# A post-norm decoder block on one NeuronCore: another order for the second half's projection tiles, weight requests and FFN products

## The chip, the cores and the metric

The kernel runs on one core of a Trainium2 chip. The metric is the device time of one execution in microseconds; before the change it is 2226.97 us, the median of three runs (2224.86 to 2243.2). Engines are called by their names in the profile: PE is TensorE, PEld its weight loads, DVE is VectorE, ACT is ScalarE, POOL is GpSimd and SP is the queue that issues all DMAs.

## What is computed

x is (4, 1024, 512), the context (4, 2048, 512). Three sublayers, each followed by a layer norm over the 512 features:

```python
x = layernorm(x + attention(x))          # q, k, v each from two linear maps, 32 head slots of 16; then one projection, wo
x = layernorm(x + xattn(x, ctx, fside))  # see below
x = layernorm(x + ffn(x))                # x rounded to 8-bit integers, times a ternary 512 x 512 matrix, + bias

# xattn: of the 1024 rows of x, rows 0..511 are h (z1h) and rows 512..1023 are c (z1c)
xp = concatenate([z0h, z1h], axis=2)                  # h shifted by one column
out = uss + conv(xp, weight, kernel 2) + bias         # (2048, 512) weights for each of two taps, uss is the context
it, ot, gt, ft = sigmoid, sigmoid, tanh, sigmoid of the four quarters of out
ct = ft * z0c + it * gt                               # z0c: c shifted by one column
ht = ot * tanh(ct)
return concatenate([ht, ct], axis=1)
```

So the convolution contracts over the 512 rows of h and needs all of them; c is needed only for the elementwise product with the gate ft.

## The kernel before

All fp32 products are made as three matmuls of high and low parts (`product3`). The program has four stages: `combine` and `project` make q, k and v, `attend` does the attention with TensorE nearly always busy, and `finish` does everything from the output projection on. Only `finish` (from about 1751 us of the span) and two lines of loads for it are touched.

`finish` treats the four batches in two pairs (p = 0, 1; bi = 0, 1 within a pair). A batch has TT = 8 row tiles t of 128 rows; KC = 4, so tiles t 0..3 are h and t 4..7 are c. For each pair it does:

- **Projection** (`wo_stage`): 16 tiles of 12 matmuls, in the order of positions `pos` that `wo_tile` maps to (bi, t). The left operand is in two buffers `o_hi`/`o_lo`, one half of each for bi = 0 and one for bi = 1, each half holding four tiles; `load_o`/`next_o` load a half (1 MB high, 1 MB low). Results go to six PSUM banks (`WO_BANKS`). VectorE adds x (to which GpSimd has added the bias, `add_wob`) and computes the statistics (`start_norm`: three operations), GpSimd the inverse deviation (`inv_std`), ScalarE applies the norm (`apply`). y, the tile between them, has a ring of four.
- **The convolution's rows** (`first_term`, `last_term`, `high_parts`, `low_parts`): from each h tile the minimal-filtering form of a two-tap convolution makes three half-width operands, each in two parts (`x_wino`). `tmp` uses the buffers of gate 0 and 1 in between.
- **Convolution** (`convs`): CONVS = 16 sets s. Set s belongs to m = s // 4 (which 128 rows) and gate g = s % 4; it has 4 channel blocks c of 9 matmuls (`conv_block`), and needs 1.5 MB of weights in one of two buffers (`load_w`). VectorE adds the result to the context in `gates` (two operations of 1024 columns), ScalarE does the sigmoid or tanh. After g = 2 the new c and after g = 3 the new h are made and normalised (keys "c", "h"); then the next context (`load_ctx`) may come in.
- **FFN**: 16 blocks q (`ffn_tile`). VectorE rounds (`rounded`), ScalarE makes integers (`integers`), TensorE transposes (`turn`), ScalarE copies (`copy_turned`), TensorE multiplies (`ffn`, bank 7), VectorE reads it (`out_of_ffn`), ScalarE normalises into the output (`apply_ffn`). In set s VectorE does `out_of_ffn(s-6)` and `rounded(s-4)` before the set's own sums. TensorE does `turn(s-5)` before the last channel block of set s and `ffn(s-5)` after it. x of the second pair is loaded into the place of block q when block q is out (`next_x`).

Six FFN blocks (10 to 15) of the first pair are left when its sets end; they are fitted into the projection of the second pair. The tables at the head of `finish` say where: `ORDER[p]` is the order in which all engines but TensorE take the tiles, `FFN_AT` says before which entry of it an `ffn_part` stands, `FFN_SLOT` the same for TensorE's positions, `X_AT` when GpSimd adds the bias to an x tile. `place` numbers all normalisations in program order, which is how the ring's users agree.

Each engine runs its own instructions in order and waits on semaphores. On SP too each request waits in order, so a request stands behind all waits ahead of it.

## Time and profile before

| | us |
|---|---|
| median of three runs | 2226.97 |
| lowest, highest | 2224.86, 2243.2 |
| the profiled execution | 2238.76 |
| its span, first to last instruction | 2236.8 |
| TensorE, VectorE, ScalarE, GpSimd busy | 2120.3, 1658.8, 1314.4, 487.8 |
| projection and rows, first pair | 1752.6 to 1807.3 |
| sets 0 to 15, first pair | 1807.3 to 1972.4 |
| projection, rows, FFN blocks 10 to 15 | 1974.5 to 2038.8 |
| sets 0 to 15, second pair | 2038.8 to 2200.6 |
| end | 2236.8 |

The profile is of one execution. A row of a timeline gives the start in us from the span's start, the duration, the engine, the line, the operation with output and inputs, and in brackets the engine's idle time before it with what ended it. Matmuls overlap, so a group's duration is a little more than their pace. A landing is counted from the request to the arrival of the last byte.

### The profile page before, as it was taken

To read this page: it belongs to the slowest core of one execution; us is meant where nothing else is said; L and a number is where in the kernel's file an instruction comes from. 1 tells how busy PE (TensorE), PEld (TensorE's weight loads), DVE (VectorE), ACT (ScalarE), POOL (GpSimd) and SP (SyncE) were. 2 spreads that over 40 slices of the span, in tenths; PEclk is the share of its full clock that TensorE was granted. 3 is DMA by queue.
4 is the path that set the end of the run, shared out by engine and by line. 5 is a ranking of instruction groups with operands and counts; after the bars stand their busy time and mean duration, and the time that the engine had idled before them with its cause. 6 is when DMAs were issued, how large, how long until landed. Compare 5 with 4: busy or idle time off the path is not lost. (4 is left out here: it accounts for less than half of the span.)

```text
span 2236.8 us, 40038 instructions
## 1 busy us (share of the span) xinstructions
PE 2120.3 (95%) x11304; PEld 1190.4 (53%) x11304; DVE 1658.8 (74%) x1725; ACT 1314.4 (59%) x2429; POOL 487.8 (22%) x972
## 2 busy tenths in 40 slices
PE   8999996999999999999999999999999979987995
PEld 3788883444444444444444444444443667766773
DVE  3333326888999999999999999999995357785776
ACT  0121120777888888888888888888887233443344
POOL 0000000112121221221221221221221533464234
PEclk9999995999999999999999999999998789999997
DMA  4355547354565664664665664654654646753562
GB/s 155 95 168 150 151 149 97 59 131 105 112 138 100 125 138 101 124 138 100 125 138 101 124 138 101 124 138 101 124 130 158 245 168 264 258 195 140 220 231 76
DMA packets 205963, 315.20 MB, mean 141 GB/s; under 512 B 105169, under 2 KB 105169, under 8 KB 193617
## 3 DMA queue, kind: packets, MB, share of 16 engines
q1 hardware_dynamic: 205904, 314.47, 54.2%
q8 instruction: 31, 0.51, 0.1%
q14 instruction: 28, 0.22, 0.0%
HBM read 211.06 MB, written 101.19 MB: 140 GB/s over the span
## 5 line engine op out<-in xcount | busy, mean ns | idle before, releaser
L517 DVE TENSOR_REDUCE neg_max<-psum 128x1 f32<-128x1024 f32 x1024 | 1205.2, 1220 | 143.9 <-PE psum L405 143.6
L497 ACT ACTIVATE probs<-psum 128x512 f32<-128x512 f32 x2048 | 1066.3, 604 | 326.3 <-PE psum L423 323.8
L423 PE MATMUL psum<-q_op,k_op 50*128 50x512 f32 x2048 | 765.7, 456 | 6.2 <-ACT probs L497 3.9
L423 PEld LDWEIGHTS psum<-q_op,k_op 50*128 50x128 f32 x2048 | 359.1, 194 | 593.5 <-ACT probs L497 569.9
L405 PE MATMUL psum<-k_op,q_op 48*128 48x512 f32 x2048 | 633.2, 489 | 21.6 <-DMA k_op<-qk_parts_dram 14.1
L432 PE MATMUL psum<-probs,v_op 128*32 128x512 f32 x4096 | 557.7, 617 | 1.7
L405 PEld LDWEIGHTS psum<-k_op,q_op 48*128 48x128 f32 x2048 | 390.0, 315 | 51.9 <-DVE neg_max L517 19.3
L149 PE MATMUL psum<-x_wino,conv_w 128*128 128x512 f32 x1152 | 287.5, 407 | 29.5 <-DMA conv_w<-conv_w_parts_dram 14.9
L149 PEld LDWEIGHTS psum<-x_wino,conv_w 128*128 128x128 f32 x1152 | 222.2, 195 | 81.3 <-issue 32.6
L567 POOL CAST neg_max_parts<-neg_max 128x8 fp32r<-128x8 f32 x128 | 24.5, 191 | 809.3 <-DVE neg_max L517 809.3
L432 PEld LDWEIGHTS psum<-probs,v_op 128*32 128x32 f32 x4096 | 83.1, 108 | 132.5 <-issue 74.3
L230 ACT ACTIVATE qk_parts<-psum,qk_bias 128x512 fp32r<-128x512 f32 x64 | 44.1, 689 | 166.0 <-PE psum L149 166.0
L243 DVE SCALAR_TENSOR_TENSOR qk_parts<-psum,qk_bias,qk_parts 128x512 fp32r<-128x512 f32 x64 | 48.0, 750 | 120.1 <-ACT qk_parts L230 120.1
L557 POOL COPY v_op<-values 128x256 f32 (+1 forms) x64 | 25.5, 398 | 455.3 <-issue 344.6
L1049 ACT ACTIVATE x<-y,neg_mean_rstd,rstd 128x512 f32<-128x512 f32 x64 | 52.1, 816 | 103.6 <-POOL neg_mean_rstd L963 103.6
L149 PE MATMUL psum<-x_hi,w_hi 128*128 128x512 f32 x256 | 101.9, 398 | 5.0 <-ACTq L224 5.0
L1323 DVE TENSOR_TENSOR gates<-psum,gates 128x1024 f32<-128x1024 f32 x32 | 38.9, 1216 | 90.3 <-PE psum L149 90.3
L149 PE MATMUL psum<-x_lo,w_hi 128*128 128x512 f32 x256 | 101.7, 397 | 0.0
L149 PE MATMUL psum<-x_hi,w_lo 128*128 128x512 f32 x256 | 101.6, 397 | 0.0
L1105 ACT ACTIVATE gates<-gates,conv_bias 128x1024 f32<-128x1024 f32 x32 | 36.7, 1151 | 93.3 <-DVE gates L1326 93.2
L683 POOL TENSOR_TENSOR o_raw<-o_raw,recips 128x512 f32<-128x512 f32 x32 | 41.0, 1282 | 175.9 <-DMA recips<-recips_dram 175.9
L958 POOL TENSOR_TENSOR var_eps<-mean_var,eps 128x1 f32<-128x1 f32 x96 | 30.8, 321 | 200.9 <-DVE mean_var L1228 200.7
(98 smaller groups left out, 1655.4 us busy)
## 6 DMA issues: line engine op xcount, KB each, us to landing
q_op<-qk_parts_dram SPq DMA_DIRECT2D x384, 128.0 KB, 4.0
conv_w<-conv_w_parts_dram SPq DMA_DIRECT2D x32, 1536.0 KB, 7.9
qk_parts_dram<-qk_parts SPq DMA_DIRECT2D x128, 256.0 KB, 3.1
k_op<-qk_parts_dram SPq DMA_DIRECT2D x384, 64.0 KB, 3.8
conv_w_parts_dram<-conv_w_parts SPq DMA_DIRECT2D x16, 1536.0 KB, 6.1
attended_dram<-out SPq DMA_DIRECT2D x64, 256.0 KB, 2.1
attended_parts_dram<-o_parts SPq DMA_DIRECT2D x128, 128.0 KB, 2.2
gates<-in_ctx_dram SPq DMA_DIRECT2D x32, 512.0 KB, 4.3
```

The lines of the kernel that those rows point to most:

```text
L149: mm = nc.tensor.matmul(out, left, right, start=(first and i == 0), stop=(last and i == n - 1))
L230: nc.scalar.activation(parts[j % 4][:, 0, :], bank[j % 6], ACT.Identity, bias=qk_bias[:, j // KC, j % KC:j % KC + 1]).then_inc(qk_hi, 1)
L243: nc.vector.scalar_tensor_tensor(out=parts[j % 4][:, 1, :], in0=bank[j % 6], scalar=qk_bias[:, j // KC, j % KC:j % KC + 1], in1=parts[j % ...
L405: return nc.tensor.matmul(s1_bank[t % 2][:, lane * HALF:(lane + 1) * HALF], qop[i][r, b, t:S:QT], kop[i][r, b, :], start=True, stop=True)
L423: nc.tensor.matmul(s2_bank[cell % RING], kop[i][r, j // 2, n // 2 * P:(n // 2 + 1) * P], qop[i][r, j // 2, j % 2 * HALF:(j % 2 + 1) * HALF ...
L432: mm = nc.tensor.matmul(pv_bank[32 * j:32 * j + 32, :], vop[k % 2][:, j // 2 * QT + kt, :], probs[n % DEEP][:, j, :], start=(n == 0), stop ...
L497: nc.scalar.activation(probs[n % DEEP][:, j, :], s2_bank[cell % RING], ACT.Exp, scale=SCALE).then_inc(exp_done, 1)
L517: nc.vector.tensor_reduce(mx[b][:, t:t + 1], s1_bank[t % 2][:], AX_X, ALU.max, negate=True).then_inc(maxed, 1)
L683: nc.gpsimd.tensor_tensor(norm["o"][:], norm["o"][:], norm["den"][:], ALU.mult).then_inc(norm["o_made"], 1)
L1049: A.activation(dst, y[r][:], ACT.Identity, bias=nmr[:, r:r + 1], scale=rstd[:, r:r + 1]).then_inc(normed, 1)
L1105: A.activation(gin[:, g, :, :], gin[:, g, :, :], ACT.Tanh if g == 1 else ACT.Sigmoid, bias=cb[:, col:col + 1]).then_inc(gate_out, 1)
L1323: steps.done(V.tensor_tensor(both, bank[4 + s % 2].rearrange("p (b i a) -> p b i a", b=2, a=1).broadcast_to([P, 2, HF, 2]), both, ALU.add))
```

## The change

- `WO_TILES` replaces the arithmetic of `wo_tile`: positions 0 to 7 are now the h tiles, (0,0), (0,1), (1,0), (1,1), (0,2), (1,2), (0,3), (1,3), and 8 to 15 the c tiles. `load_o` loads the h half first, the first x tiles loaded in `attend` are those of the new positions 0 to 3, and `next_o` asks for the halves of the c tiles when seven and eight tiles are multiplied (before: four and eight). Row making moves to the entries behind each h tile. `WO_BANKS` is turned so that the banks of set 0 are free after thirteen tiles; TensorE waits for thirteen tiles before set 0 and sixteen before set 1. A wait is added on VectorE before c is used.
- Sets 0 and 1 run one after the other (before: blocks 0 to 2 of both, then block 3 of both).
- SP asks for the weights of set s + 2 before the contexts that follow set s - 1 (before: before the contexts that follow set s, ahead of the next weights).
- TensorE multiplies FFN block s - 6 behind the first channel block of set s (before: block s - 5 behind set s).
- Between the pairs single tables (`O_AT`, `R_AT`, `TURN_AT`, `FFN_AT`, `COPY_AT`) replace `ffn_part` and `FFN_SLOT`, so that rounding, turning, copying and multiplying a block each have a position of their own. ScalarE copies block 11 within set 15.

```diff
+    WO_BANKS = (4, 2, 3, 5, 0, 1)
+    WO_TILES = ((0, 0), (0, 1), (1, 0), (1, 1), (0, 2), (1, 2), (0, 3), (1, 3)) + \
+        tuple((bi, t) for bi in range(2) for t in range(KC, TT))
+    ORDER = (tuple(range(TILES)), (0, 1, 2, 3, 4, 5, 8, 9, 6, 10, 7, 11, 12, 13, 14, 15))
...
+    FFN_AT = ({}, {1: 10, 2: 11, 5: 12, 6: 13, 7: 14, 8: 15})
...
 def next_o(p, n):
-    sp.wait_ge(wo_full, p * TILES + 4 * n - 4)
+    sp.wait_ge(wo_full, p * TILES + (4 * n - 4 if n < 2 else n + 5))
...
 def convs(p):                                   # SP
     for s in range(CONVS):
-        m, g = s // 4, s % 4
-        if p * CONVS + s + 2 < 2 * CONVS and s + 2 < CONVS:
+        if s + 2 < CONVS:
             sp.wait_ge(conv_full, p * CONVS + s + 1)
             load_w(p * CONVS + s + 2)
+        if s > 0:
+            next_ctx(p, s - 1)
...
-        if m < KC - 1 and g == 2:
-            sp.wait_ge(cell_made, p * KC + m + 1)
-            load_ctx(p, m + 1, 2)
...
                 next_o(0, 2)
-                for pos in range(8, TILES):
-                    load_x(0, *wo_tile(pos))
...
 def convs(p):                                   # TensorE
-    for s in range(2):
-        pe.wait_ge(wo_out, p * TILES + TILES - 1 + s)
-        pe.wait_ge(cw_in[s], (p * CONVS // 2 + 1) * DMA)
-        for c in range(KC - 1):
-            conv_block(p, s, c)
-    for s in range(2):
-        conv_block(p, s, KC - 1)
-    for s in range(2, CONVS):
+    for s in range(CONVS):
         n = p * CONVS + s
-        pe.wait_ge(gate_in, n - 1)
+        if s < 2:
+            pe.wait_ge(wo_out, p * TILES + 13 + 3 * s)
+        else:
+            pe.wait_ge(gate_in, n - 1)
         pe.wait_ge(cw_in[n % 2], (n // 2 + 1) * DMA)
         for c in range(KC):
+            if c == 1 and s >= 6:
+                ffn(p, s - 6)
             if c == KC - 1 and s >= 5:
                 turn(p, s - 5)
             conv_block(p, s, c)
-        if s >= 5:
-            ffn(p, s - 5)
+    turn(p, CONVS - 5)
...
 def wo_stage(p):                                # VectorE
     for i, pos in enumerate(ORDER[p]):
-        if i in FFN_AT[p]:
-            ffn_part(p - 1, FFN_AT[p][i])
+        if i in O_AT[p]:
+            out_of_ffn(p - 1, O_AT[p][i])
+        if i in R_AT[p]:
+            rounded(p - 1, R_AT[p][i])
         out_of_wo(p, pos)
...
+        if wino_of(p, i - 2) is not None:
+            low_parts(p, wino_of(p, i - 2))
+        if wino_of(p, i - 1) is not None:
+            first_term(p, wino_of(p, i - 1))
```

How the order moves, first on SP at the first pair's projection (`o_hi` and `o_lo` are the attention rows, `x` the residual tiles, `o_parts` the last attention results). Before:

```order
L655 DMA recips<-recips_dram 128x1x512 [waits recips_out]
L697 DMA o_hi<-attended_parts_dram 128x4x512 [waits wo_full]
L697 DMA o_lo<-attended_parts_dram 128x4x512
L839 DMA x<-in_x_dram 128x512 x8
L670 DMA attended_parts_dram<-o_parts 32x2x512 [waits o_lo_made]
L670 DMA attended_parts_dram<-o_parts 32x2x512 x3
L697 DMA o_hi<-attended_parts_dram 128x4x512 [waits wo_full]
L697 DMA o_lo<-attended_parts_dram 128x4x512
L852 DMA conv_w<-conv_w_parts_dram 128x3072 [waits conv_w_stored]
L852 DMA conv_w<-conv_w_parts_dram 128x3072
```

After:

```order
L656 DMA recips<-recips_dram 128x1x512 [waits recips_out]
L848 DMA x<-in_x_dram 128x512 x8
L698 DMA o_hi<-attended_parts_dram 128x4x512 [waits wo_full]
L698 DMA o_lo<-attended_parts_dram 128x4x512
L698 DMA o_hi<-attended_parts_dram 128x4x512 [waits wo_full]
L698 DMA o_lo<-attended_parts_dram 128x4x512
L671 DMA attended_parts_dram<-o_parts 32x2x512 [waits o_lo_made]
L671 DMA attended_parts_dram<-o_parts 32x2x512 x3
L861 DMA conv_w<-conv_w_parts_dram 128x3072 [waits conv_w_stored]
L861 DMA conv_w<-conv_w_parts_dram 128x3072
```

The eight x tiles now stand ahead of the first attention rows, and the two pairs of attention rows stand next to each other ahead of the store.

SP again, from the first weights requested within the sets (sets 2 and 3 of the first pair) on; `gates` is the context. Before:

```order
L852 DMA conv_w<-conv_w_parts_dram 128x3072 [waits conv_full] x2
L697 DMA o_hi<-attended_parts_dram 128x4x512 [waits wo_full,o_parts_stored]
L697 DMA o_lo<-attended_parts_dram 128x4x512
L852 DMA conv_w<-conv_w_parts_dram 128x3072 [waits conv_full]
L848 DMA gates<-in_ctx_dram 128x2x512 [waits cell_made]
L848 DMA gates<-in_ctx_dram 128x2x512 [waits var_made,tanh_made]
L852 DMA conv_w<-conv_w_parts_dram 128x3072 [waits conv_full]
L848 DMA gates<-in_ctx_dram 128x2x512 [waits h_made]
L848 DMA gates<-in_ctx_dram 128x2x512 [waits var_made]
L852 DMA conv_w<-conv_w_parts_dram 128x3072 [waits conv_full]
L697 DMA o_hi<-attended_parts_dram 128x4x512 [waits wo_full]
L697 DMA o_lo<-attended_parts_dram 128x4x512
```

After:

```order
L861 DMA conv_w<-conv_w_parts_dram 128x3072 [waits conv_full] x2
L698 DMA o_hi<-attended_parts_dram 128x4x512 [waits wo_full,o_parts_stored]
L698 DMA o_lo<-attended_parts_dram 128x4x512
L861 DMA conv_w<-conv_w_parts_dram 128x3072 [waits conv_full] x2
L857 DMA gates<-in_ctx_dram 128x2x512 [waits cell_made]
L857 DMA gates<-in_ctx_dram 128x2x512 [waits var_made,tanh_made]
L861 DMA conv_w<-conv_w_parts_dram 128x3072 [waits conv_full]
L857 DMA gates<-in_ctx_dram 128x2x512 [waits h_made]
L857 DMA gates<-in_ctx_dram 128x2x512 [waits var_made]
L698 DMA o_hi<-attended_parts_dram 128x4x512 [waits wo_full]
L698 DMA o_lo<-attended_parts_dram 128x4x512
L861 DMA conv_w<-conv_w_parts_dram 128x3072 [waits conv_full] x2
```

The third and fourth weight requests (sets 4 and 5) now follow each other with no context between them, and so on by four.

TensorE in sets 6 and 7 of the first pair (`tern` is the FFN's matrix, `ident` the identity of a turn). Before:

```order
L149 MATMUL psum<-x_wino,conv_w 128x512 [waits conv_w_in0,gate_in]
L149 MATMUL psum<-x_wino,conv_w 128x512 x26
L1136 MATMUL psum<-ident,x_int 128x128 [waits tp_out,xi_made]
L1136 MATMUL psum<-ident,x_int 128x128 x3
L149 MATMUL psum<-x_wino,conv_w 128x512 x9
L1146 MATMUL psum<-tern,x_int_t 128x512 [waits ffn_out,tp_out]
L1146 MATMUL psum<-tern,x_int_t 128x512 x3
L149 MATMUL psum<-x_wino,conv_w 128x512 [waits conv_w_in1,gate_in]
L149 MATMUL psum<-x_wino,conv_w 128x512 x26
L1136 MATMUL psum<-ident,x_int 128x128 [waits tp_out,xi_made]
L1136 MATMUL psum<-ident,x_int 128x128 x3
```

After:

```order
L149 MATMUL psum<-x_wino,conv_w 128x512 [waits conv_w_in0,gate_in]
L149 MATMUL psum<-x_wino,conv_w 128x512 x8
L1168 MATMUL psum<-tern,x_int_t 128x512 [waits tp_out]
L1168 MATMUL psum<-tern,x_int_t 128x512 x3
L149 MATMUL psum<-x_wino,conv_w 128x512 x18
L1158 MATMUL psum<-ident,x_int 128x128 [waits tp_out,xi_made]
L1158 MATMUL psum<-ident,x_int 128x128 x3
L149 MATMUL psum<-x_wino,conv_w 128x512 x9
L149 MATMUL psum<-x_wino,conv_w 128x512 [waits conv_w_in1,gate_in]
L149 MATMUL psum<-x_wino,conv_w 128x512 x8
L1168 MATMUL psum<-tern,x_int_t 128x512 [waits ffn_out,tp_out]
L1168 MATMUL psum<-tern,x_int_t 128x512 x3
```

The FFN product has moved from the end of a set to behind the first nine matmuls of the next.

## Rows read from the trace of the kernel before

**Rows 1.** The view of waits, TensorE, 1750 to 2237 us: in total, times, longest.
```profile
PE psum L149 <- DMA conv_w<-conv_w_parts_dram: 14.9, 5, 4.6
PE psum L1146 <- DVE y L1257: 14.7, 8, 2.0
```

**Rows 2.** Timeline of TensorE, 1800 to 1846 us: start, us, instructions, idle before.
```profile
1807.27 19.44 PE L149 MATMUL psum<-x_wino,conv_w 128*128 128x512 f32 x72 [7.99 <-DVE x_wino L1289]
1831.36 14.83 PE L149 MATMUL psum<-x_wino,conv_w 128*128 128x512 f32 x52 [4.65 <-DMA conv_w<-conv_w_parts_dram]
```

**Rows 3.** Timelines of VectorE: its first read after sets 2, 6, 10, 14.
```profile
1842.60 1.22 DVE L1323 TENSOR_TENSOR gates<-psum,gates 128x1024 f32<-128x1024 f32 x1 [13.02 <-PE psum L149]
...
1880.18 1.23 DVE L1323 TENSOR_TENSOR gates<-psum,gates 128x1024 f32<-128x1024 f32 x1 [5.95 <-PE psum L149]
...
1921.50 1.23 DVE L1323 TENSOR_TENSOR gates<-psum,gates 128x1024 f32<-128x1024 f32 x1 [4.44 <-PE psum L149]
...
1963.16 1.22 DVE L1323 TENSOR_TENSOR gates<-psum,gates 128x1024 f32<-128x1024 f32 x1 [3.89 <-PE psum L149]
...
2072.04 1.22 DVE L1323 TENSOR_TENSOR gates<-psum,gates 128x1024 f32<-128x1024 f32 x1 [11.73 <-PE psum L149]
...
2109.28 1.23 DVE L1323 TENSOR_TENSOR gates<-psum,gates 128x1024 f32<-128x1024 f32 x1 [4.45 <-PE psum L149]
...
2150.09 1.22 DVE L1323 TENSOR_TENSOR gates<-psum,gates 128x1024 f32<-128x1024 f32 x1 [4.44 <-PE psum L149]
...
2191.42 1.23 DVE L1323 TENSOR_TENSOR gates<-psum,gates 128x1024 f32<-128x1024 f32 x1 [4.45 <-PE psum L149]
```

**Rows 4.** Timeline of the DMA queue, 1855 to 1863 us: weights after two contexts.
```profile
1861.57 1.34 SPq L852 DMA_DIRECT2D conv_w<-conv_w_parts_dram  x1
```

**Rows 5.** Timeline of TensorE, 1880 to 1980 us: FFN products between sets.
```profile
1891.52 1.60 PE L1146 MATMUL psum<-tern,x_int_t 128*128 128x512 bf16 x4 [1.99 <-DVE y L1257]
1892.56 7.78 PE L149 MATMUL psum<-x_wino,conv_w 128*128 128x512 f32 x27
...
1902.53 1.04 PE L1146 MATMUL psum<-tern,x_int_t 128*128 128x512 bf16 x4
...
1911.92 1.04 PE L1146 MATMUL psum<-tern,x_int_t 128*128 128x512 bf16 x4
```

**Rows 6.** Timeline of VectorE, 1890 to 1902 us: two readings of FFN products.
```profile
1890.63 0.75 DVE L1257 SCALAR_TENSOR_TENSOR y<-psum,scale,x 128x512 f32<-128x512 f32 x1
...
1901.13 0.75 DVE L1257 SCALAR_TENSOR_TENSOR y<-psum,scale,x 128x512 f32<-128x512 f32 x1
```

**Rows 7.** Tile views, landing: o_lo issued at 1767, at 2008; then all weights.
```profile
DMA to landing us min/median/max: 7.2/7.2/7.2
...
DMA to landing us min/median/max: 13.5/13.5/13.5
...
DMA to landing us min/median/max: 6.2/7.9/16.1
```

**Rows 8.** Timelines between the pairs, TensorE 1977.60 and 2038.82, the others VectorE.
```profile
1977.60 0.60 PE L1136 MATMUL psum<-ident,x_int 128*128 128x128 bf16 x4 [2.08 <-ACT x_int L1056]
...
2024.26 0.74 DVE L1257 SCALAR_TENSOR_TENSOR y<-psum,scale,x 128x512 f32<-128x512 f32 x1
...
2029.49 0.68 DVE L1247 TENSOR_TENSOR y<-psum,x 128x512 f32<-128x512 f32 x1
...
2031.11 0.43 DVE L1284 TENSOR_TENSOR x_wino<-x,x_wino 128x256 fp32r<-128x256 f32 x1
...
2032.50 0.69 DVE L1247 TENSOR_TENSOR y<-psum,x 128x512 f32<-128x512 f32 x1
...
2037.12 0.88 DVE L1284 TENSOR_TENSOR x_wino<-x,x_wino 128x256 fp32r<-128x256 f32 x1
...
2038.82 5.83 PE L149 MATMUL psum<-x_wino,conv_w 128*128 128x512 f32 x18 [6.40 <-DVE x_wino L1289]
```

**Rows 9.** Timeline of TensorE, 2200 to 2237 us: the product of block 11.
```profile
2215.13 1.89 PE L1146 MATMUL psum<-tern,x_int_t 128*128 128x512 bf16 x4 [9.51 <-ACT x_int_t L1062]
```

More of the change, by code:

```diff
@@ L376, in slot @@
                         for t in range(KC):
-                            sp.dma_start(late["x_first"][:, t, :], x_nat[0, (KC + t) * P:(KC + t + 1) * P, :])\
+                            b, row = t // 2, t % 2 * P
+                            sp.dma_start(late["x_first"][:, t, :], x_nat[b, row:row + P, :])\
                                 .then_inc(late["x_in"], DMA)
@@ L721, in finish, with wino_of @@
     RING = 4
-    WO_BANKS = (0, 1, 4, 2, 3, 5)
-    ORDER = (tuple(range(TILES)), (0, 1, 2, 4, 5, 6, 3, 8, 9, 7, 10, 11, 12, 13, 14, 15))
-    FFN_AT = ({}, {0: 16, 3: 17, 4: 18, 6: 19, 8: 20, 11: 21})
-    FFN_SLOT = ({}, {0: 16, 3: 17, 5: 18, 7: 19, 9: 20, 11: 21})
-    X_AT = {2: 9, 6: 12, 7: 10, 9: 13, 10: 11, 11: 14, 14: 15}
+    WO_BANKS = (4, 2, 3, 5, 0, 1)
+    WO_TILES = ((0, 0), (0, 1), (1, 0), (1, 1), (0, 2), (1, 2), (0, 3), (1, 3)) + \
+        tuple((bi, t) for bi in range(2) for t in range(KC, TT))
+    ORDER = (tuple(range(TILES)), (0, 1, 2, 3, 4, 5, 8, 9, 6, 10, 7, 11, 12, 13, 14, 15))
+    O_AT = ({}, {0: 10, 1: 11, 3: 12, 4: 13, 6: 14, 7: 15})
+    R_AT = ({}, {0: 12, 1: 13, 2: 14, 3: 15})
+    TURN_AT = ({}, {4: 12, 5: 13, 6: 14, 7: 15})
+    FFN_AT = ({}, {1: 10, 2: 11, 5: 12, 6: 13, 7: 14, 8: 15})
+    COPY_AT = ({}, {1: 12, 2: 13, 3: 14, 4: 15})
+    X_AT = {2: 10, 3: 11, 4: 9, 6: 12, 7: 14, 8: 13, 9: 15}
     def wo_tile(pos):
-        return pos // 4 % 2, pos % 4 + (KC if pos < 8 else 0)
+        return WO_TILES[pos]
+    def wino_of(p, i):
+        return ORDER[p][i] if 0 <= i < TILES and ORDER[p][i] < 2 * KC else None
     def ffn_tile(q):
@@ L743, in finish @@
         for i, pos in enumerate(ORDER[p]):
-            if i in FFN_AT[p]:
-                takes("ffn", p - 1, FFN_AT[p][i] - 6)
+            if i in O_AT[p]:
+                takes("ffn", p - 1, O_AT[p][i])
             takes("wo", p, pos)
@@ L919, in _ @@
                 convs(0)
+                for n in range(CONVS, CONVS + 2):
+                    sp.wait_ge(conv_full, n - 1)
+                    load_w(n)
                 next_x(10)
@@ L922, in _ @@
                 next_x(11)
-                next_o(1, 2)
-                store(0, 11)
-                next_x(12)
-                for n in range(CONVS, CONVS + 2):
-                    sp.wait_ge(conv_full, n - 1)
-                    load_w(n)
                 sp.wait_ge(var_made, place["h", 0, KC - 1, 1] + 1)
@@ L931, in _ @@
                     load_ctx(1, 0, g)
+                store(0, 11)
+                next_x(12)
+                store(0, 12)
                 next_x(13)
-                store(0, 12)
+                next_o(1, 2)
+                store(0, 13)
+                next_x(14)
+                store(0, 14)
                 next_o(1, 3)
-                next_x(14)
-                store(0, 13)
                 next_x(15)
-                store(0, 14)
                 store(0, 15)
@@ L965, in add_wob @@
                 def add_wob(p, bi, t):
-                    pool.wait_ge(x_in[bi * TT + t], (p if bi == 0 and t >= KC else p + 1) * DMA)
+                    pool.wait_ge(x_in[bi * TT + t], (p if (bi, t) in WO_TILES[:KC] else p + 1) * DMA)
                     G.tensor_tensor(x_at(bi, t), x_at(bi, t), wob[:], ALU.add).then_inc(x_wob, 1)
@@ L1090, in wo_stage @@
                     for i, pos in enumerate(ORDER[p]):
-                        if i in FFN_AT[p]:
-                            ffn_part(p - 1, FFN_AT[p][i])
+                        if i in COPY_AT[p]:
+                            copy_turned(p - 1, COPY_AT[p][i])
+                        if i in R_AT[p]:
+                            integers(p - 1, R_AT[p][i])
+                        if i in O_AT[p]:
+                            apply_ffn(p - 1, O_AT[p][i])
                         apply(x_at(*wo_tile(pos)), "wo", p, pos)
-                        if i >= 9:
-                            high_parts(p, (i - 9) // KC, (i - 9) % KC)
-                    high_parts(p, 1, 3)
+                        if wino_of(p, i - 1) is not None:
+                            high_parts(p, wino_of(p, i - 1))
                 def convs(p):
@@ L1148, in ffn @@
                     mm.then_inc(ffn_full, 1)
-                def ffn_part(p, s):
-                    if s > CONVS:
-                        ffn(p, s - 6)
-                    if s - 5 < TILES:
-                        turn(p, s - 5)
                 def wo_stage(p):
                     for pos in range(TILES):
-                        if pos in FFN_SLOT[p]:
-                            ffn_part(p - 1, FFN_SLOT[p][pos])
-                        n = pos // 4
-                        if pos % 4 == 0:
-                            pe.wait_ge(late["o_in"][n % 2], (2 * p + n // 2 + 1) * (2 * DMA))
+                        if pos in FFN_AT[p]:
+                            ffn(p - 1, FFN_AT[p][pos])
+                        if pos in TURN_AT[p]:
+                            turn(p - 1, TURN_AT[p][pos])
+                        bi, t = wo_tile(pos)
+                        n = bi + (2 if t >= KC else 0)
+                        pe.wait_ge(late["o_in"][bi], (2 * p + n // 2 + 1) * (2 * DMA))
                         if pos >= 6:
@@ L1211, in _ @@
                 convs(1)
-                for s in range(CONVS, CONVS + 6):
-                    ffn_part(1, s)
+                for q in range(CONVS - 6, TILES):
+                    ffn(1, q)
+                    if CONVS - 4 <= q + 1 < TILES:
+                        turn(1, q + 1)
             @block.vector
```

92 lines of the change are left out of this document (49 added, 43 removed).

## The prediction

> **What bounds the kernel now.** I read the view of TensorE's waits over the last 485 us first, then the timelines of TensorE, VectorE and the DMA queue around each wait, because the diff leaves everything before 1751 us alone. In that last part TensorE has the most work, and what can be won is its idle time. Two families of waits stand out [rows 1]: 14.9 us for convolution weights in five waits, and 14.7 us for FFN rows that VectorE had not yet read in eight waits. A third is the wait for the convolution's rows: 7.99 us before the first convolution and 6.40 us before the second pair's [rows 2, 8]. Each long pause also costs clock. The 72 matmuls after the 7.99 us pause took 19.44 us [rows 2], against 16.3 at the undisturbed pace. That pace is 9.39 us for a whole set (36 convolution matmuls, a turn and an FFN product, no wait) [rows 5], of which I give 8.15 to the 36 matmuls and 2.72 to a projection tile of 12. After the 4.65 us pause 52 matmuls took 14.83 us [rows 2], 3.0 more than 52 x 0.227. So a pause of about 5 us costs 5 plus 2 to 3. I call T2, T6, T10 and T14 the end of a pair's sets 2, 6, 10 and 14 (counted from 0), which is where VectorE starts on its sums; [rows 3] hold these for both pairs: 1842.60, 1880.18, 1921.50, 1963.16, and 2072.04, 2109.28, 2150.09, 2191.42.
>
> **Step 1, first pair up to T2 (now 1842.60).** Gone: the 7.99 us wait for rows, because they are made from tiles 0 to 7 while tiles 8 to 15 still multiply; and the 4.65 us weight wait with its slow 3.0 us. Sets 0 and 1 now run one after the other, so the weights of set 2 are asked for 8.15 us before they are needed rather than when both are nearly done. New: both halves of the attention rows are now asked for only when seven and eight tiles are done, so tile 8 waits for them. TensorE starts at 1752.6, loses 3 us to the clock as now, ends tile 6 at about 1774.8 and tile 7 at 1777.5. The second of the two requests leaves at 1775.3. The nearest rows for its landing are 7.2 us (little else in flight) and 13.5 us (amid weights) [rows 7]. At 1775 the eight x tiles, now asked for ahead of it, have mostly landed, so I take 7.2: TensorE goes on at 1782.5, after 5.0 us idle. Eight tiles take 21.8 us and the clock 2.5: 1806.8. VectorE has then emptied thirteen tiles by about 1800 (a tile with its rows takes it 3.0 us, from one reading to the next in [rows 8]), so the convolution follows at once. Three sets at 8.15: 1831.3. **Gain 11.3** (5.0 if landing takes 13.5).
>
> **Step 2, sets 3 to 6 of either pair (T2 to T6).** Now 37.6 and 37.2 us [rows 3]. Two weight waits lie in the first, since the queue stood behind the context's waits (weights issued at 1861.57 [rows 4], where set 4 had ended at 1842.6 + 16.5 = 1859.1). With weights ahead: 8.2 + 8.2 + 8.4 + 9.4 = 34.2. Gains 3.4 and 3.0. In the first pair one request for set 7 comes right behind 2 MB of attention rows. Weights land in 6.2 to 16.1 us, 7.9 in the middle [rows 7]; this one I put at 10.6, which is 1.2 beyond the 9.39 it has. The context is asked for later, but has 8 us or more. **Gain 5.2.**
>
> **Step 3, FFN product behind the first channel block.** T6 to T10 and T10 to T14 take, over both pairs, 41.3, 41.7, 40.8 and 41.3 us [rows 3], together 165.1, against 4 x 37.56 without waits. Two things fill the difference: the pauses before the FFN product, and the clock after one of them (1.60 us for four matmuls, then 7.78 for 27) [rows 5]. VectorE reads the first FFN row 10.45 us after T (1890.63) and the next 20.95 after it (1901.13) [rows 6], and needs 0.75 for each. The product now stands 2.1 us later on TensorE, at T + 11.5 and T + 20.9. So the first pause is covered (11.2 against 11.5), and the second is left with 0.8, at most about 2.0. With 1.1 on average: 4 x 38.65 = 154.6. **Gain 10.5.**
>
> **Step 4, between the pairs (T14 = 1963.16 to T2 = 2072.04: 108.9 us).** TensorE turns one more FFN block and is free at T + 14.4, as now (the turn at 1977.60 [rows 8]). From here VectorE sets the pace, because the last FFN products (blocks 12 to 15) each wait for it, and the product of block 15, which stands ahead of projection tile 8, waits for VectorE's reading of block 14. How long until then? VectorE begins at about T + 21.3, a little after the 20.95 of [rows 6]. Before that reading it has 4 FFN rows and 6 projection tiles at 1.6 us, 4 roundings at 1.0 to 1.5, 4 low parts and 5 first terms (1.4 a pair) [rows 8], and the 0.75 of the reading: 27.6 us, so T + 48.9 with no wait. Scaled from now: it reads block 15 at 2024.26, T + 61.1 [rows 8], with one FFN row and five tiles more and three low-and-first pairs fewer, so 5.3 us more work: T + 55.8. I take 51.7, nearer to the work, since ScalarE and GpSimd make it wait about 3 us. Then TensorE, idle for 6 us, has one product (0.9), eight tiles (21.8), 2.5 us of clock, and about 1 for x tiles 14 and 15, which can be loaded only after those readings: T + 78. Three sets: T + 102.5. So the convolution of the second pair begins no earlier than now (T + 75.7); the gain is the weight wait and its clock, less 2.3. **Gain 6.4**; with 48.9, 9.2, and with 55.8, 2.3.
>
> VectorE and GpSimd get in each other's way here: one low part took 0.43 us and another 0.88 [rows 8]; I have taken the short one. By the Trainium skill (SBUF — State Buffer, section Who interferes with whom) a VectorE instruction with two SBUF inputs and a GpSimd instruction that reads SBUF shut each other out for a whole instruction. That rule speaks against the change, since the rows are now made while GpSimd still adds biases to the later tiles. By it the four low parts before the reading cost 0.45 more each and the sum would be 2193.4; by the row it is 2191.6.
>
> **Step 5, the end.** The product of block 11 waits until 2215.13 for ScalarE's copy [rows 9], which stood behind two normalisations. It is now made within the last set, so the product waits only for VectorE, to 2213.1. **Gain 2.0.**
>
> **Sum:** 11.3 + 5.2 + 10.5 + 6.4 + 2.0 = 35.4 us. The profiled execution took 2238.8 us (span 2236.8), 0.5% above the median of 2227.0; from it 2203.4, from the median 2191.6. I forecast 2191.6 as the median.
>
> **Rivals.**
> *Attention rows land late (2202).* They come as two times 2 MB, now one behind the other. For: 13.5 us in one row. Against: that one was amid weight loads. Step 1 loses 6.3 and step 4 about 4. Chance 0.13.
> *The FFN product gains nothing (2202).* VectorE's second reading is delayed as much as the product is. For: after the change VectorE would find the product only 3 us into the set. Against: T + 20.95 is not paced by TensorE in [rows 6]. Chance 0.10.
> *Between the pairs TensorE alone sets the pace (2180).* If VectorE, ScalarE and GpSimd keep up, the stage is T + 14.4, 43.5 for tiles, 6.4 for products and turns and 2 of clock: T + 66.3, 11.7 sooner. For: VectorE's work after the change is the same amount. Against: each product 12 to 15 waits for a VectorE reading. Chance 0.17.
> *Slower (2245).* Between the pairs the copies stand ahead of ScalarE's normalisations and wait for turns that stand after three tiles on TensorE, while tiles wait for VectorE and it for ScalarE. If every such hop is exposed and an iteration takes 10 us instead of my 5, the eight iterations add 40 and the rest 13. It decides from 35 us more than in step 4. Against: each hop by itself is 1 to 3 us. Chance 0.04.
> *The queue change does nothing (2202):* weights take over 9.4 us (the longest took 16.1 [rows 7]) when context lands with them, so that being asked for earlier is eaten up. Against: the middle value is 7.9, well below that. Chance 0.04.
> The forecast itself has 0.52.
>
> **Numbers.** The likeliest case with its bounds (step 4: +2.8 and -4.1, step 3: +4 and -3.6, clock +/-3) spans 2183 to 2201. To hold 8 in 10 I go to 2179 (the quick case) and 2207 (late rows with a slow step 4). About 1%, 22 us, is what a measurement of this kernel tells from no change, so 2204.7 is the limit. Faster by more: 0.52 + 0.17 + half of 0.27 = 0.83. Within 1%: 0.13. Slower: 0.04.
>
> **What would show it.** Right: no wait for rows before either convolution, no weight wait before set 2, sets 0 to 2 in 24.5 us, TensorE idle for about 5 us before tile 8 of the first pair and for about 6 us before tile 8 of the second, T6 to T10 near 38.5. Wrong: a pause longer than 8 us before tile 8, T6 to T10 at 41, or a second convolution that begins later than T + 84.

## The result and the profile after

The changed kernel takes 2198.15 us, median of four (2196.87 to 2200.61), beside 2231.28 for the kernel before (2224.86 to 2243.2): a ratio of 0.985, 95% interval 0.980 to 0.989. The profiled execution took 2196.87 us (span 2194.9); before it was 2238.76 (span 2236.8), 41.9 more. Of these 41.9, 6.7 lie ahead of everything that was changed: the first projection matmul starts at 1745.91 us instead of 1752.57. In the 13 profiles of the changed kernel and its variants this start lies anywhere from 1744.8 to 1759.9, although ahead of it at most the addresses of four loads differ between them. So I compare the last stage alone, from that matmul to the end: 484.2 us before, 449.0 now, 35.2 less. The forecast was 35.4.

VectorE's first reads after sets 2, 6, 10 and 14 (start, duration, line, operation, count, idle before), as in [rows 3]:

```profile
1822.05 1.23 DVE L1341 TENSOR_TENSOR gates<-psum,gates 128x1024 f32<-128x1024 f32 x1 [5.68 <-PE psum L149]
...
1856.22 1.22 DVE L1341 TENSOR_TENSOR gates<-psum,gates 128x1024 f32<-128x1024 f32 x1 [3.86 <-PE psum L149]
...
1895.15 1.23 DVE L1341 TENSOR_TENSOR gates<-psum,gates 128x1024 f32<-128x1024 f32 x1 [3.86 <-PE psum L149]
...
1934.72 1.22 DVE L1341 TENSOR_TENSOR gates<-psum,gates 128x1024 f32<-128x1024 f32 x1 [3.86 <-PE psum L149]
...
2039.68 1.22 DVE L1341 TENSOR_TENSOR gates<-psum,gates 128x1024 f32<-128x1024 f32 x1 [5.68 <-PE psum L149]
...
2073.85 1.23 DVE L1341 TENSOR_TENSOR gates<-psum,gates 128x1024 f32<-128x1024 f32 x1 [3.86 <-PE psum L149]
...
2112.58 1.23 DVE L1341 TENSOR_TENSOR gates<-psum,gates 128x1024 f32<-128x1024 f32 x1 [3.86 <-PE psum L149]
...
2151.32 1.22 DVE L1341 TENSOR_TENSOR gates<-psum,gates 128x1024 f32<-128x1024 f32 x1 [3.86 <-PE psum L149]
```

Their differences, with S for the first projection matmul and E for the end of the span, give the table on which all that follows rests (us):

| | S-T2 | T2-T6 | T6-T10 | T10-T14 | T14-T2 | T2-T6 | T6-T10 | T10-T14 | T14-E | sum |
|---|---|---|---|---|---|---|---|---|---|---|
| before | 90.03 | 37.58 | 41.32 | 41.66 | 108.88 | 37.24 | 40.81 | 41.33 | 45.38 | 484.2 |
| after | 76.14 | 34.17 | 38.93 | 39.57 | 104.96 | 34.17 | 38.73 | 38.74 | 43.58 | 449.0 |
| gain | 13.9 | 3.4 | 2.4 | 2.1 | 3.9 | 3.1 | 2.1 | 2.6 | 1.8 | 35.2 |

The waits of TensorE from 1745 us to the end (line waited at, for what: us in total, times, longest), against [rows 1]:

```profile
PE psum L1168 <- DVE y L1274: 18.7, 7, 6.6
PE psum L1158 <- ACT x_int L1074: 10.6, 4, 5.1
PE psum L149 <- DMA o_lo<-attended_parts_dram: 5.5, 1, 5.5
...
PE psum L149 <- DMA conv_w<-conv_w_parts_dram: 1.1, 1, 1.1
```

Weights cost 1.1 us where they cost 14.9. The wait for VectorE's reading of FFN rows (line 1274 now) is not smaller in all, but other ones make it up, as the timeline of TensorE shows:

```profile
1745.91 0.47 PE L149 MATMUL psum<-wo_hi,o_hi 128*128 128x512 f32 x1 [1.64 <-PEq L330]
...
1773.41 0.80 PE L149 MATMUL psum<-wo_hi,o_hi 128*128 128x512 f32 x1 [5.46 <-DMA o_lo<-attended_parts_dram]
...
1857.28 2.32 PE L149 MATMUL psum<-x_wino,conv_w 128*128 128x512 f32 x9 [1.09 <-DMA conv_w<-conv_w_parts_dram]
...
1917.82 1.02 PE L1168 MATMUL psum<-tern,x_int_t 128*128 128x512 bf16 x4 [1.81 <-DVE y L1274]
...
1949.15 0.61 PE L1158 MATMUL psum<-ident,x_int 128*128 128x128 bf16 x4 [5.08 <-ACT x_int L1074]
...
1988.04 1.48 PE L1168 MATMUL psum<-tern,x_int_t 128*128 128x512 bf16 x3 [6.56 <-DVE y L1274]
...
2095.68 1.02 PE L1168 MATMUL psum<-tern,x_int_t 128*128 128x512 bf16 x4 [0.96 <-DVE y L1274]
```

The reader sees the new idle before tile 8 (5.46), the one weight wait left (1.09, set 7 of the first pair), at most one FFN pause, of 1.0 to 1.8, in each block of four sets where there were one or two of 1.0 to 2.0, the turn of block 12 that waits 5.08 but starts at T14 + 14.43, as before (1977.60 less 1963.16), and product 15 at T14 + 53.3, idle for 6.56.

### The profile page after: what moved, and what is told of

Its sections match the earlier page's. It is cut to its first block and busy times, and to the rows that moved or that the text cites. A ratio compares the mean times of both kernels' runs of the same rounds, so it can differ in the third digit from the quotient of the medians.

```text
span 2194.9 us, 40044 instructions
## 1 busy us (share of the span) xinstructions
PE 2100.3 (96%) x11290; PEld 1181.7 (54%) x11304; DVE 1660.1 (76%) x1725; ACT 1314.6 (60%) x2429; POOL 487.7 (22%) x972
## 5 line engine op out<-in xcount | busy, mean ns | idle before, releaser
L406 PE MATMUL psum<-k_op,q_op 48*128 48x512 f32 x2048 | 630.6, 488 | 21.7 <-DMA k_op<-qk_parts_dram 14.3
L149 PE MATMUL psum<-x_wino,conv_w 128*128 128x512 f32 x1152 | 275.2, 395 | 1.1 <-DMA conv_w<-conv_w_parts_dram 1.1
L149 PEld LDWEIGHTS psum<-x_wino,conv_w 128*128 128x128 f32 x1152 | 214.6, 188 | 47.1 <-issue 1.5
L1067 ACT ACTIVATE x<-y,neg_mean_rstd,rstd 128x512 f32<-128x512 f32 x64 | 52.3, 817 | 110.4 <-POOL neg_mean_rstd L979 110.4
```

The lines of the kernel that those rows point to most:

```text
L149: mm = nc.tensor.matmul(out, left, right, start=(first and i == 0), stop=(last and i == n - 1))
L406: return nc.tensor.matmul(s1_bank[t % 2][:, lane * HALF:(lane + 1) * HALF], qop[i][r, b, t:S:QT], kop[i][r, b, :], start=True, stop=True)
L1067: A.activation(dst, y[r][:], ACT.Identity, bias=nmr[:, r:r + 1], scale=rstd[:, r:r + 1]).then_inc(normed, 1)
```

## The experiments

Medians and ratios stand beside runs of the kernel before on the same chip (2231 to 2237 us); `thin_adds` and `copy_in_tail` ran once each. Because of the wandering start, mechanisms are read from the stages of the profiles, one profile of each version. Where nothing in them was changed, the three stages from T2 to T14 of a pair repeat to 0.3 us from run to run. S to T2 does so only to 2.3 us (76.1 to 78.4), mostly by the clock it starts at. T14 to T2 took 104.96 after the change and 105.0 to 105.2 in `ctx_first`, `copy_in_tail` and `stats_first`, but 106.44 and 106.15 in `rows_early` and `stats_and_rows`, whose edits lie in the first pair too. Most of that difference has arisen by product 15 (T14 + 54.9 and 54.8 for 53.3), and its cause is open. So differences of 1.5 us in this stage prove nothing.

### One part undone at a time

**Contexts ahead of the weights again** (`ctx_first`), in SP's `convs`; the added line ends a step:

```diff
-                        if s > 0:
-                            next_ctx(p, s - 1)
...
+                        next_ctx(p, s)
```

> The changed kernel with one part undone: SP again asks for a set's contexts ahead of the next weights. Theory (the order of the queue is worth what step 2 says): the weights of sets 5 and 6 are asked for about 2.8 us later (when the contexts' waits are over, T2 + 11 and T2 + 19) and both sets wait 1.5 to 2.5 us, so T2 to T6 takes about 37.4 instead of 34.2 us in each pair, 6.5 us in all, near 2205. Rival (landing has room enough either way): T2 to T6 stays within 0.5 us of 34.2 and the time at 2198.

Measured: T2 to T6 36.24 and 36.45, the first pair's T6 to T10 40.88 (38.93), and 0.5 and 0.7 more in the two T10 to T14; 7.8 us in all over the last stage. Median 2211.8, ratio 0.992 (0.988 to 0.996). Its waits of TensorE, and two requests of the DMA queue (T2 is 1832.11 here):

```profile
PE psum L149 <- DMA conv_w<-conv_w_parts_dram: 8.3, 9, 1.8
```

```profile
1839.45 3.62 SPq L857 DMA_DIRECT2D gates<-in_ctx_dram  x2
1843.12 0.46 SPq L861 DMA_DIRECT2D conv_w<-conv_w_parts_dram  x1
```

The weights go out at T2 + 11.0, right behind the contexts, and there are nine short waits where the kernel before had five, up to 4.6 us long. Each pair loses less in its first four sets than expected (2.2, not 3.2), and the rest falls into later sets. The theory holds, the rival falls. The median lies 13.6 us above the changed kernel's; what exceeds the 7.8 was not traced (in this profile the last stage begins 9.9 us later).

**Product behind the set again** (`ffn_behind_set`), in TensorE's `convs` (the product of block 10 then stands behind set 15, so `FFN_AT` loses its entry):

```diff
-                            if c == 1 and s >= 6:
-                                ffn(p, s - 6)
...
+                        if s >= 5:
+                            ffn(p, s - 5)
```

> The changed kernel with one part undone: TensorE multiplies FFN block s - 5 behind set s instead of block s - 6 behind the first channel block. Theory: the pause of 2 us in three of four sets is back, T6 to T10 and T10 to T14 take 41.3 us instead of 38.7 to 39.6, 9 us in all, near 2207. Rival (VectorE's later stages set the period, the place of the product is nothing): under 3 us in all, near 2200.

Measured: the four periods 40.79, 41.61, 40.79 and 40.79, 8.0 us more than the 155.97 of the changed kernel. Median 2213.8, ratio 0.993 (0.990 to 0.996). A pause of 2.0 to 2.2 us is back once in four sets, not in three of four. The wait grows from 18.7 us in 7 to

```profile
PE psum L1168 <- DVE y L1274: 34.7, 14, 7.6
```

The place of the product is worth 2.0 us per four sets. The rival that it gains nothing is out.

**Sets 0 and 1 side by side again** (`sets_together`), TensorE's `convs` as in the removed lines of the diff above, but still with thirteen and sixteen emptied tiles before sets 0 and 1.

> The changed kernel with one part undone: sets 0 and 1 run blocks 0 to 2 of both, then block 3 of both. Theory: the weights of set 2 are asked for only 2.5 us before they are needed, TensorE waits 4 to 5 us and loses 2 to 3 us of clock, so the time from the first convolution matmul to T2 grows from 24.5 to about 31 us in each pair: 13 us in all, near 2211. Rival (the earlier gain of the first stage came from the rows alone): at most 2 us a pair, near 2202.

Measured: T14 to T2 takes 112.42 (7.5 more). From the first convolution matmul to T2 it takes 31.5 us in the first pair, where the changed kernel takes 24.7: 6.8 more, about as expected. Median 2209.3, ratio 0.992 (0.990 to 0.995). The wait in its timeline of TensorE:

```profile
1834.23 11.15 PE L149 MATMUL psum<-x_wino,conv_w 128*128 128x512 f32 x41 [4.96 <-DMA conv_w<-conv_w_parts_dram]
```

So about half of the first stage's gain of 13.9 comes from running the two sets one behind the other. Between the pairs the same part brings 7.5, yet the stage gained only 3.9: the rest of the change costs 3.6 there.

No run undid the order of the tiles alone, but the profiles before and after show what it did in the first pair. The convolution starts at S + 51.45 instead of S + 54.70, 3.25 us sooner. Of this 2.72 is the clock over the first eight tiles (22.05 us instead of 24.77, see step 1 below). That leaves 0.5: the wait of 7.99 us before the convolution has given way to one of 5.46 before tile 8 and 2.0 us of slow clock behind it (the second eight tiles take 23.95 instead of 21.95). The larger part of its worth comes later. Behind its start the convolution needs 24.69 us to T2 instead of 35.33, and of these 10.6 the sets one behind the other explain 6.8. The other 3.8 is near the 3.1 (19.44 - 16.3) that the clock behind the 7.99 us wait had cost.

**The copy of block 11 behind the last set again** (`copy_in_tail`), ScalarE's `convs` with `if 4 <= s < CONVS - p`; its `ffn_part` makes the copy instead.

> The changed kernel with one part undone: ScalarE copies block 11 of the last pair behind set 15 instead of within it. Theory of step 5: the product of block 11 waits for that copy behind two normalisations, T14 to the end takes 45.4 instead of 43.6 us. Rival: VectorE's reading sets that end anyway, 43.6.

Measured: T14 to the end 45.40, all else within 0.2. It was 45.38 before the change. The theory holds.

### What ends last ahead of the first convolution

The forecast said that VectorE would be done long before TensorE. The profile after says otherwise. VectorE's timeline (two separate places), then GpSimd's:

```profile
1764.32 0.44 DVE L1296 TENSOR_TENSOR gates<-x 128x256 f32<-128x256 f32 x1 [10.00 <-ACT x L1067]
...
1787.04 0.90 DVE L1303 TENSOR_TENSOR x_wino<-x,x_wino 128x256 fp32r<-128x256 f32 x1
...
1796.24 0.69 DVE L1264 TENSOR_TENSOR y<-psum,x 128x512 f32<-128x512 f32 x1
```

```profile
1758.78 1.28 POOL L684 TENSOR_TENSOR o_raw<-o_raw,recips 128x512 f32<-128x512 f32 x1 [4.99 <-DMA recips<-recips_dram]
...
1786.37 1.29 POOL L983 TENSOR_TENSOR x<-x,wo_bias 128x512 f32<-128x512 f32 x1
```

VectorE idles for 10.00 us because the first tile's statistics stand, on GpSimd, behind the last attention normalisation, which itself waits 4.99 us for a DMA. Then it takes 3.43 us for a tile with its row (1785.43 to 1788.87) and reads tile 12, the thirteenth, only at 1796.24. That reading ends at 1796.93, 0.4 us before the first convolution matmul, at 1797.36 or S + 51.5. Two chains of nearly equal length end there: TensorE with its pause for attention rows, and GpSimd with VectorE.

**The rows early** (`rows_early`), first pair only:

The h tiles come in the order (0,0) to (0,3), (1,0) to (1,3), the x tiles and the order of the rows follow, SP asks for the first attention rows of the c tiles ahead of the eight x tiles again, and

```diff
-    sp.wait_ge(wo_full, p * TILES + (4 * n - 4 if n < 2 else n + 5))
+    sp.wait_ge(wo_full, p * TILES + (4 * n - 4 if p == 0 or n < 2 else n + 5))
```

> The changed kernel, in the first pair only with tiles (0,0) to (0,3) ahead of (1,0) to (1,3), so that the attention rows of the c tiles are asked for after four and eight tiles. Theory (VectorE paces the first projection, the pause of TensorE before tile 8 is covered): the pause of 5.5 us goes, but the convolution starts at most 1 us sooner, 51 us behind the first tile instead of 51.7, since it still waits for thirteen emptied tiles: near 2197. Rival (the pause is on the path, as step 1 counted it): 5.5 us and 2.5 us of clock come off, near 2190.

**Statistics first** (`stats_first`), GpSimd:

```diff
-                normalise(pool, nc, norm, PAIRS - 1)
-                wo_stage(0)
+                wo_stage(0, range(3))
+                normalise(pool, nc, norm, PAIRS - 1)
+                wo_stage(0, range(3, TILES))
```

> The changed kernel, in which GpSimd does the statistics of the first three projection tiles ahead of the last attention normalisation (it idles 5.0 us there, and VectorE waits 10.0 us behind it). Theory (two chains of the same length end at the first convolution: the attention rows with TensorE's pause, and GpSimd with VectorE): alone it changes nothing, convolution 51.7 us behind the first tile, 76.1 to T2. Rival (the statistics alone were the bound): the convolution starts about 5 us sooner.

**Both** (`stats_and_rows`):

> Both at once: the statistics first, and the first pair's tiles ordered so that the attention rows of the c tiles are asked for after four and eight tiles. Theory of two chains: only both together help; GpSimd and VectorE begin 5 us sooner and TensorE has no pause, so the convolution starts about 46.5 us behind the first tile instead of 51.7 and T2 comes 71 to 73 us behind it instead of 76.1. Rival (VectorE's own work is the bound however early it starts): convolution at 51, T2 at 76 to 78.

Measured. `rows_early`: the 5.5 us pause is gone, the convolution starts at S + 51.03, and T2 is even 2.0 us later (78.14). `stats_first`: S to T2 77.72, which is what other runs with a start at the low clock take without the edit (77.8 and 78.4): nothing. Its VectorE now reads the thirteenth tile by S + 45.9, while TensorE reaches the convolution only at S + 53.0, so the other chain is the bound:

```profile
1794.61 0.69 DVE L1266 TENSOR_TENSOR y<-psum,x 128x512 f32<-128x512 f32 x1 [0.35 <-PE psum L149]
```

In `rows_early` it is the other way round: TensorE ends its tiles at S + 46.4 and VectorE that reading at S + 50.7. Both: the convolution at S + 46.23, T2 at 72.49. TensorE's timelines of `rows_early`, then of `stats_and_rows`, at the first convolution:

```profile
1799.41 15.92 PE L149 MATMUL psum<-x_wino,conv_w 128*128 128x512 f32 x59 [4.58 <-issue]
```

```profile
1804.29 11.03 PE L149 MATMUL psum<-x_wino,conv_w 128*128 128x512 f32 x41 [2.42 <-issue]
```

In `rows_early` the pause has only moved, from before tile 8 to before the convolution; there the slow clock behind it (0.52 on average over the next 5 us) is paid on the path (from there to T2 it takes 78.14 - 51.03 = 27.1 us, where the changed kernel takes 76.14 - 51.45 = 24.7). The medians are 2200.0, 2202.8 and 2194.4, the ratios 0.986, 0.985 and 0.982, too close for times alone. The stage settles it: two chains, and only both edits together shorten it. Over the whole last stage `stats_and_rows` takes 446.5 us, 2.5 less than the changed kernel and not 3.7, because T14 to T2 took 1.2 more.

**GpSimd's additions cut to one column** (`thin_adds`) on top of `stats_and_rows`. It leaves out most of the bias addition from tile 4 of the first pair on, so it shows a cost and is no version to use:

```diff
-  G.tensor_tensor(x_at(bi, t), x_at(bi, t), wob[:], ALU.add)
+  G.tensor_tensor(x_at(bi, t)[:, 0:1], x_at(bi, t)[:, 0:1], wob[:, 0:1], ALU.add)
```

> The run with statistics and rows first, but GpSimd adds the projection's bias only to the first column of each tile (which leaves out the rest of that addition from tile 4 of the first pair on). Theory (GpSimd's full-width additions lengthen VectorE's instructions beside them): VectorE's first low part takes 0.4 to 0.5 us in each row instead of 0.7 to 0.9, a tile with its row 2.9 us instead of 3.4, and the first convolution starts 44 to 45 us behind the first tile instead of 46.2. Rival (they don't touch each other, TensorE sets the pace of 43.5 plus a pause): low parts and the start stay.

Measured: the convolution starts at S + 43.6, S to T2 is 68.33 instead of 72.49, T14 to T2 103.26 instead of 106.15, and the first pair's T10 to T14 38.75 instead of 39.59. Product 15 starts at T14 + 52.3 instead of 54.8. VectorE's first low part, in the costliest groups by line and form over 1745 to 1815 us (count, then busy, mean ns, idle before), in `stats_and_rows` and in `thin_adds`:

```profile
L1310 DVE TENSOR_TENSOR x_wino<-x,x_wino 128x256 fp32r<-128x256 f32 x8 | 6.6, 823 | 2.6 <-ACT x_wino L1110 2.6
```

```profile
L1310 DVE TENSOR_TENSOR x_wino<-x,x_wino 128x256 fp32r<-128x256 f32 x8 | 3.8, 477 | 0.9 <-ACT x_wino L1110 0.9
```

The same instruction takes 823 ns beside full-width additions and 477 without. In the rows above it began 0.6 us before GpSimd's addition ended (1787.66) and ended 0.3 us after it, as if held until then. By the Trainium skill (SBUF — State Buffer, Who interferes with whom) a VectorE instruction with two SBUF inputs and a GpSimd instruction that reads SBUF lock each other out for a whole instruction; these rows agree. The run also cuts GpSimd's own work, so the 2.6 us of the start (46.2 to 43.6) belong to both effects; they were not told apart. At 43.6 TensorE's 16 tiles (43.5) are the bound.

### Between the pairs

**Product of block 15 later** (`last_product_later`): `FFN_AT` has `10: 15` for `8: 15`, nothing else.

> The changed kernel with the product of FFN block 15 behind projection tile 9 of the second pair instead of ahead of tile 8. Theory (TensorE waits 6.6 us for VectorE there and VectorE then 5.5 us for tile 8: one waits for the other in turn, but the attention rows of tile 8, asked for 10 us before, hide behind the same pause): tile 8 starts about 2.5 us sooner, T14 to T2 takes about 102.5 instead of 105.0. Rival A (VectorE's work alone is the bound): no gain, 105.0. Rival B (the product alone is the bound): 5.5 us, 99.5.

**And the attention rows of tile 8 sooner** (`product_and_rows2`): with product 15 as in the last run, `next_o(1, 2)` stands ahead of `store(0, 12)` and `next_x(13)` too.

> The same, and SP asks for the attention rows of tile 8 of the second pair ahead of the store and the x tile that it stood behind, about 3 us sooner. Theory: tile 8 starts 5 to 5.7 us sooner, T14 to T2 about 99.5 to 100. Rival (VectorE's work alone is the bound): 105.0, with VectorE's 5.5 us wait for tile 8 replaced by one later.

Measured: T14 to T2 104.80 and 104.48 (104.96). Both theories missed; the numbers are those of the rival, by which VectorE's work is the bound. TensorE's timelines, of `last_product_later`, then of `product_and_rows2`:

```profile
1986.85 0.80 PE L149 MATMUL psum<-wo_hi,o_hi 128*128 128x512 f32 x1 [5.58 <-DMA o_lo<-attended_parts_dram]
```

```profile
1990.24 0.53 PE L149 MATMUL psum<-wo_hi,o_hi 128*128 128x512 f32 x1 [2.77 <-DMA o_lo<-attended_parts_dram]
...
2006.93 0.50 PE L149 MATMUL psum<-wo_hi,o_hi 128*128 128x512 f32 x1 [2.98 <-DMA o_lo<-attended_parts_dram]
```

The pause of 6.56 us for VectorE becomes one of 5.58 for attention rows, which had hidden behind it; with those asked for sooner it shrinks to 2.77, and another of 2.98 opens before tile 12.

**All of it, both attention requests ahead** (`rows_early_both`): the statistics and the rows as above, product 15 later, and for the second pair (0,3) ahead of (1,2) on TensorE with `ORDER[1]` to match. SP asks for the attention rows of its c tiles after six and eight tiles instead of seven and eight, and

```diff
+                next_o(1, 2)
                 store(0, 12)
                 next_x(13)
+                next_o(1, 3)
                 store(0, 13)
```

> Everything that helped: statistics first, attention rows early in the first pair, product of block 15 behind tile 9; and in the second pair both requests for attention rows ahead of the store and x tile that they stood behind, with tiles (0,2), (0,3), (1,2), (1,3) in this order so that the first may leave one tile sooner. Theory (between the pairs the pause for tile 12's attention rows, 3.0 us, took the place of the pause for the product): T14 to T2 falls to 101 or 102 us from the 104.5 of the run with only the first request moved, S to T2 stays 72.5. Rival (VectorE with GpSimd and ScalarE paces that stage by itself): T14 to T2 stays at 104 to 105 and TensorE waits for emptied banks instead.

**And the scale's five small instructions later** (`constants_later`): `if p == 0 and i == 14` for `i == 11`.

> The fastest version so far, with VectorE's five small instructions on the scale (1.2 us in all, ahead of its reading of tile 12) moved behind tile 14. Theory (the first convolution waits for VectorE's reading of the thirteenth tile): convolution 45.1 us behind the first tile instead of 46.3, S to T2 near 71.4 instead of 72.5, the rest as before, median near 2189. Rival (TensorE's tiles end no sooner than that, 43.5 us and a slow start): convolution stays at 46.3, S to T2 at 72.5.

Measured. `rows_early_both`: T14 to T2 103.97, median 2190.6, ratio 0.980 (0.976 to 0.984). No pause for attention rows is left, but TensorE waits 4.78 us for an emptied bank. So the rival held: here VectorE, with GpSimd and ScalarE, sets the pace. `constants_later`: the convolution starts at S + 45.22, as expected, and S to T2 is 70.02, 1.4 better than expected, since the clock held behind the pause of 1.42 us; T14 to T2 is 101.63, which I had not expected; median 2195.0, where near 2189 was expected, ratio 0.981 (0.978 to 0.984). Timelines of TensorE at the bank's wait, and its window of 5 us (busy time and count by engine, granted clock, DMA), of `rows_early_both`, then of `constants_later`:

```profile
2007.46 0.77 PE L149 MATMUL psum<-wo_hi,o_hi 128*128 128x512 f32 x1 [4.78 <-DVE y L1271]
```

```profile
2007.40:2012.40 5.00, 4.94 (x12) 3.95 (x13) 3.74 (x8) 1.63 (x2) 4.69 (x10) 0.50 0.44 157
```

```profile
1998.15 0.47 PE L149 MATMUL psum<-wo_hi,o_hi 128*128 128x512 f32 x1 [4.81 <-DVE y L1271]
```

```profile
1998.10:2003.10 5.00, 4.95 (x15) 3.95 (x16) 3.73 (x8) 1.63 (x2) 4.70 (x10) 0.66 0.52 157
```

Of the 2.3 us between the two, 1.0 had arisen by this wait (T14 + 62.66 and + 61.63) and 1.3 behind it, with a mean clock of 0.50 in one and 0.66 in the other after nearly the same pause. The 1.0 is within what this stage varies by without an edit, and I can't assign it; VectorE's first terms (`first_term`) took 579 ns on average in the one and 498 in the other.

Against the changed kernel the last version's final stage is 439.9 us to 449.0, 9.1 less in one profile each. The timed medians show 3 us, and the ratio intervals overlap with the changed kernel's. That it is faster is likely, not shown.

## Why the prediction was right, and where by luck

**Sum.** 35.4 forecast, 35.2 measured over the last stage; the medians moved by 33.1, to 2198.15 in place of 2191.6. Of the 6.6 between, 4.3 is the kernel before, whose median is 2231.28 with a fourth run where the forecast started from 2226.97, and 2.3 is the gain. Against the profiled before the forecast was 2203.4, and the profiled run took 2196.87; these 6.5 are the start, 6.7 sooner. That 35.4 and 35.2 agree so well is in part luck: 2.7 of the 35.2 are the clock at the start of the stage (next paragraph), which no part of the change was meant to touch. Without them 32.5 are left, near the 33.1 of the medians.

**Step 1 (11.3, measured 13.9).** The pause before tile 8 was right: 5.46 for 5.0, landing in 7.7 for 7.2. The failed step is "VectorE has then emptied thirteen tiles by about 1800", 7 us ahead: it was 0.4 us ahead. Two terms were missing, VectorE's 10.00 us idle at the start, behind GpSimd, and 3.43 us for a tile instead of 3.0. That the answer was near is luck: the chain I left out was as long as the one I counted. The excess of 2.6 is the clock at the start, which "loses 3 us to the clock as now" took as fixed. The first eight tiles took 22.05 us instead of 24.77, and without these 2.7 the stage gained 11.2 for the 11.3 forecast. By windows, just ahead of the pause of 1.63 us before the first projection matmul and just behind it, before the change:

```profile
1747.90:1750.90 3.00, 3.00 (x16) 0.39 (x8) 0.00 (x0) 0.10 (x1) 0.00 (x0) 0.50 0.00 0
1752.50:1757.50 5.00, 4.93 (x12) 3.90 (x13) 0.00 (x0) 0.00 (x0) 5.00 (x8) 0.50 0.84 262
```

And after it:

```profile
1741.20:1744.20 3.00, 3.00 (x16) 0.45 (x12) 0.00 (x0) 0.56 (x2) 0.00 (x0) 0.58 0.00 0
1745.90:1750.90 5.00, 4.99 (x22) 4.13 (x23) 0.00 (x0) 0.00 (x0) 5.00 (x5) 1.00 0.81 271
```

Both attentions end at half clock. In the profile after, the clock has risen to full just before the pause (a mean of 0.58 over the last 3 us, 1.00 over the last 0.4), in the profile before only well behind it. The variants fall on both sides too: those whose first projection matmul took 0.76 or 0.77 us (`sets_together`, `ffn_behind_set`, `stats_first`, `product_and_rows2`) need 23.4 to 24.9 us for the first eight tiles (two of the four behind a pause of about 6 us), those with 0.47 need 21.8 to 22.1.

**Steps 2 and 3 (15.7, measured 6.5 + 9.15 = 15.65).** T2 to T6 is 34.17 in each pair, forecast 34.2. The wait of set 7's weights behind the attention rows came as forecast (1.09 for 1.2), but it lies behind T6. It costs next to nothing there, since T6 to T10 is 38.93 with it and 38.73 in the second pair without it. It took the place of that period's FFN pause. The variants have the same wait, of 0.5 to 1.2 us, and 38.7 to 39.0 (all but `ctx_first` and `ffn_behind_set`). The four periods took 155.97, forecast 154.6; the pauses are 0.96 in the second pair, near the 0.8 worked out, and 1.81 in the first pair's T10 to T14, where GpSimd already adds biases to the next pair's tiles (`thin_adds`: 38.75, without them).

**Step 4 (6.4, measured 3.9).** VectorE, with GpSimd and ScalarE, does set the pace: `last_product_later`, `product_and_rows2` and `rows_early_both` each took a wait of TensorE away and found another. The mis-sized term is T14 to product 15: 51.7 forecast, 53.3 measured. From there to the convolution 26.9 for 26.3. The work count gave 48.9. Part of what it left out is GpSimd's hold on VectorE, for example 1.52 us for a rounding (1965.40) that takes 0.47 elsewhere, while a GpSimd addition ran from 1965.26 for 1.37. Without most of GpSimd's additions product 15 came 2.6 us sooner (`thin_adds`), but that run also spares GpSimd the work, so the hold alone has no measured size.

**Step 5 (2.0, measured 1.8)** was right in mechanism and size (`copy_in_tail`).

**Rivals.** Late attention rows: no, 7.7 us. The product gains nothing: no, 8.0. TensorE alone between the pairs: no, the convolution came at T14 + 80.3, not 66.3. The slower case: no. The queue does nothing: no, 7.8 (the forecast gave no sum for that rival's 2202). Undone alone, the queue's order cost 7.8 us where 6.5 was expected, the place of the product 8.0 for 9, the two sets 14.3 for 13, the copy 1.8 for 1.8.

## What to carry to other kernels

When a change removes the wait that ends a stage, list every chain that ends at the same point and give each its own sum, from its first idle on; the one that is left out decides how much of the next edit arrives. A pause that goes may only move, and if it moves from covered work to the path, its clock cost is then paid in full (`rows_early`). Compare stages between fixed events, not whole spans, when the part ahead of the change wanders by more than the gain.
